# Twelve single buffers for the pair mask, and 28 pair additions moved from the edge stage to the expert block

## The chip, the cores and the metric

The kernel runs on one core of one Trainium2 chip. Its parts are named as the profile names them: TensorE (PE, with PEld for its weight loads), VectorE (DVE), ScalarE (ACT), GpSimd (POOL) and SyncE (SP), which here only issues transfers. The metric is the device time of one execution in microseconds; the median of three runs is compared.

## The reference

Input: x (1250 rows of 512), 20000 edges (src, dst) with features and weights. Four blocks, each added to x. They are given here without the layer norms ahead of each.

```python
x = x + L0_gnn(norm(x), src, dst, ...)       # messages on 20000 edges, segment_sum into 1250 nodes
x = x + L0_ffn(norm(x), ...)                 # 64 experts, sign routing, splines: x + y in it
x = x + L1_gnn(norm(x), [src, dst], ...)     # 4 blocks: sparse attention and a two-layer MLP
x = x + L1_ffn(norm(x), ...)                 # ternary weights, SwiGLU
```

Inside L0_ffn (its input is the normalised x, called z below, so that x + z + y is what comes out):

```python
xn = (x - mu) * rsqrt(var + EPS) * gamma + beta
tidx = best tile of the best cluster by sign agreement
y = einsum(spline(sigmoid(xn @ Wd[tidx])), Wu[tidx]) * scale[tidx]
return x + y
```

Inside each attention of L1_gnn:

```python
scores = einsum('ehd,ehd->eh', q[src], k[dst])          # one score per edge and head
attn = softmax of the scores over the edges of one src
out = segment_sum(attn * v[dst], src)
```

An edge may occur more than once. The kernel computes this attention densely, over 1250 x 1250, with a mask: the logarithm of how often the pair (src, dst) occurs, and a huge negative number where it does not.

## The kernel before

**Order of the stages**, with the time in the profiled execution: input projection (to 90 us), edge stage (90 to 549), node_update (to 589), expert_norm (590 to 626), route (to 665), experts (665 to 955), the first rows stage (956 to 1120), then four rounds of attention and MLP and the last FFN, to 2903. Every stage is a block in which each engine has its own list of instructions in a fixed order, written by hand; between engines there are only semaphores.

**The pair counts.** The 20000 edges lie in 160 tiles (ET) of 125. For each tile one indirect transfer of POOL adds 125 counts (`late_cnt`, at `late_idx`) to a 1250 x 1250 array in HBM. There are two such arrays, `pairs0` and `pairs1`, used in turn, and an addition waits for the one two before it (`pair_adds`, line 572; it issues at line 580). Their sum is the count. The 160 additions are spread: 68 in the edge stage (EARLY_ADDS, of which 60, PACED_ADDS, by group), 14 in node_update, 78 in experts; `late_adds` (line 585) issues part k of the table LATE.

**Edge stage.** 40 groups of 4 edge tiles. POOL fetches node rows for a group two ahead (L339) and then issues its share of additions (L580). VectorE makes messages and one-hots (L427), TensorE gathers them by a one-hot product (L539).

**expert_norm.** ScalarE makes z = X * rstd + shift for ten row tiles (L800). POOL adds z to X (L733, X is then x + z). VectorE takes statistics of z and makes xf from it (L760, L763, L765).

**experts.** Weights stream from HBM on SP's queue. TensorE computes the down products, ScalarE and VectorE the splines, TensorE the up products, and the results are stored as y_d (L1063, ten issues). POOL issues the 78 additions, waits for y_stored and for all 160 additions, and gathers the rows of y_d (L1075, ten transfers). For each gathered tile VectorE adds it, scaled, to X (L1376) and takes statistics (L1379 to L1386), ScalarE makes `first_rows` (L1269, L1272).

**First rows stage** (`rows_stage`, `source == "first"`, `masks` true). TensorE: a conditioned row norm, then 24 units, q and k (12 of each, by columns 500, 374, 376, three passes of four matmuls each, L1432), then v by ten row tiles (L1441). Unit n of q or k is finished by ScalarE (`take`, L1769, L1774) and VectorE (`finish`, k: L1884); a unit's bank is free after that, and two banks alternate. Beside it the mask of ten row tiles is built and stored in `mask_d`:

- SP loads the two count tiles (`load_pairs`, L142 and L143, 112 and 13 rows), into `pair_c` and `pair_m`, four buffer pairs in turn by the table MASK_SET; a reload waits until the mask in the place is stored.
- VectorE, behind `finish(n)` where n is in COUNT_AT or COVER_AT: the sum and its maximum (`count`, L1890), then 1e30 where it is 0 (L1896) and max(count, 1) (L1897).
- ScalarE, behind `take(n)` by LN_AT: the logarithm (L1779).
- POOL subtracts (L1642): mask = -(1e30 where empty) + log, with the sign turned; SP stores it (`store_mask`).

SP also stores x and the normalised rows at the stage's beginning (`x_d`, `g_d`, 2.5 MB each); ScalarE waits for both before unit 12, whose k overwrites the place of `first_rows`. The conditioning weights, bvo and wv are loaded by `late` in the middle. VectorE splits wk into high and low before unit 12 (L1840).

Of the kernel before, what the change touches and what calls it, by code (L numbers as in the profile page):

```python
# [34 lines left out]
EARLY_ADDS = 68  # L35
PACED_ADDS = 60
# [3 lines left out]
BIG = 1.0e30  # L40
# [530 lines left out]

LATE = (EARLY_ADDS, EARLY_ADDS + 14, ET)

# [136 lines left out]
def expert_norm(nc, T, A, xf, sc, sgnT, sigs, pairs):  # L710

    tsum = T.E.tsum
    with ExitStack() as ctx:
        sb = lambda n, s, d=F32: ctx.enter_context(nc.sbuf_tensor(n, s, d))
        z = sb("z", [P, NT, D]); gam = sb("gam", [P, D]); bet = sb("bet", [P, D])
        shift = sb("en_shift", [P, NT])
        tsg = sb("tsg", [128, NX, KD])
        csum = sb("csum", [128, NCL, KD])
        names = ("gb_in stats_s std_s step z_ready z_added mid xf_ready turned signed csummed sign_step sigs_ready "
                 "scored sc_ready")  # L720
        with Stage(nc, names) as (gb_in, stats_s, std_s, step, z_ready, z_added, mid, xf_ready, turned, signed,
                                  csummed, sign_step, sigs_ready, scored, sc_ready):
            with nc.Block() as block:
# [5 lines left out]
                @block.gpsimd  # L729
                def _(pool):  # L730
                    for t in range(NT):
                        pool.wait_ge(z_ready, t + 1)
                        nc.gpsimd.tensor_tensor(T.X[:, t, :], T.X[:, t, :], z[:, t, :], ALU.add).then_inc(z_added, 1)  # L733

                @block.vector
                def _(dve):
# [10 lines left out]
                    v.scalar_tensor_tensor(shift[:], T.mv[:, :, 0], -1.0, T.rstd[:], ALU.mult, ALU.mult).then_inc(stats_s, 1)  # L747
# [41 lines left out]
                def _(act):  # L789
# [9 lines left out]
                    for t in range(NT):  # L799
                        s.activation(z[:, t, :], T.X[:, t, :], ACT.Identity, bias=shift[:, t:t + 1],  # L800
                                     scale=T.rstd[:, t:t + 1]).then_inc(z_ready, 1)
# [196 lines left out]
def experts(nc, T, A, R, xs_d, y_d, pairs, mask_d, x_d, g_d, place):  # L998

    with ExitStack() as ctx:  # L1000
# [23 lines left out]
                 "c_in c_made sin_s c_turned c_copied c_prod c_z c_h c_done")  # L1024
        with Stage(nc, names) as (x_in0, x_in1, x_in2, x_in3, x_in4, tab_in, tab_high, tab_low, cleared, turned, xt_act, xt_dve,
# [4 lines left out]
                                  c_in, c_made, sin_s, c_turned, c_copied, c_prod, c_z, c_h, c_done):  # L1030
# [8 lines left out]
            with nc.Block() as block:  # L1039
                @block.sync  # L1040
                def _(sp):
# [19 lines left out]
                    for t in range(NS_T):  # L1061
# [3 lines left out]
                                 A["L1_gnn_wq"][0:1].rearrange("a c d -> (a c) d")).then_inc(rows_in, 16)  # L1065
                    sp.wait_ge(rows_in, 64)

                @block.gpsimd
                def _(pool):
# [14 lines left out]
                    late_adds(pool, nc, T, pairs, 1)  # L1084
# [120 lines left out]
                def _(act):  # L1205
# [70 lines left out]
                def _(dve):  # L1276
# [113 lines left out]
def expert_layer(nc, T, A, xs_d, y_d, pairs, mask_d, x_d, g_d, place):  # L1390
    class R:
        pass
    with ExitStack() as ctx:
        sb = lambda n, s, d=F32: ctx.enter_context(nc.sbuf_tensor(n, s, d))
        R.slot = sb("r_slot", [P, NT], I32); R.scale = sb("r_scale", [P, NT])
        R.ring = ctx.enter_context(nc.sbuf_tensor("w_ring", [128, RG, WG, D], F32, side="right"))
# [3 lines left out]
        with ExitStack() as c2:  # L1400
            xf = c2.enter_context(nc.sbuf_tensor("xf", [P, NT, D], F32)); sc = c2.enter_context(nc.sbuf_tensor("sc", [P, NT, NX + NCL], F32))
            with ExitStack() as c3:
                sgnT = c3.enter_context(nc.sbuf_tensor("sgnT", [128, KD, N], BF16))
                sigs = c3.enter_context(nc.sbuf_tensor("sigs", [128, KD, NX + NCL], BF16))
                expert_norm(nc, T, A, xf, sc, sgnT, sigs, pairs)
# [45 lines left out]
class Map:  # L1451
# [4 lines left out]
    def __init__(self, nc, base):  # L1456
# [29 lines left out]
        self.pair_c = [at(f"pair_c{s}", 154240 + 10048 * s + 1536 * (s // 2), [P, N]) for s in range(4)]  # L1486
        self.pair_m = [at(f"pair_m{s}", 159264 + 10048 * s + 1536 * (s // 2), [P, N]) for s in range(4)]
# [8 lines left out]
MASK_TURN = tuple(MASK_SET[:t].count(MASK_SET[t]) for t in range(NT))  # L1496


def rows_stage(nc, T, M, source, sink, g_d, x_d, loads, late, bias, bqk, bvo, last=False, pairs=None, mask_d=None):
# [11 lines left out]
             "pair_in0 pair_in1 pair_in2 pair_in3 summed_up empty floor logd mask_made mask_out0 mask_out1 mask_out2 mask_out3")  # L1511
    with Stage(nc, names) as (cw_ready, cw_next, b_in, a_in, w_in, v_in, a_high, a_cut, b_high, b_cut, v_high, v_cut,
# [4 lines left out]
                              pair_in0, pair_in1, pair_in2, pair_in3, summed_up, empty, floor, logd, mask_made,  # L1517
                              mask_out0, mask_out1, mask_out2, mask_out3):
        pair_in, mask_out = (pair_in0, pair_in1, pair_in2, pair_in3), (mask_out0, mask_out1, mask_out2, mask_out3)
# [16 lines left out]
        with nc.Block() as block:  # L1536
            @block.sync
            def _(sp):
# [3 lines left out]
                def load_pairs(t):  # L1542
                    k = MASK_SET[t]
                    if MASK_TURN[t] >= 1:
                        sp.wait_ge(mask_out[k], 32 * MASK_TURN[t])
                    wide(sp, M.pair_c[k][:], counts[0][t * P:(t + 1) * P, :], pair_in[k])
                    wide(sp, M.pair_m[k][:], counts[1][t * P:(t + 1) * P, :], pair_in[k])

                def store_mask(t):
                    sp.wait_ge(mask_made, t + 1)  # L1550
                    wide(sp, mask_d[t * P:(t + 1) * P, :], M.pair_c[MASK_SET[t]][:], mask_out[MASK_SET[t]])
# [16 lines left out]
                if masks:  # L1568
                    load_pairs(0)
                    load_pairs(1)  # L1570
                    wide(sp, x_d.rearrange("(t p) d -> p t d", p=P), T.X, T.spilled)
                    wide(sp, g_d.rearrange("(t p) d -> p t d", p=P), M.first, T.spilled)
                    sp.wait_ge(T.spilled, 64)
                    load_pairs(2)
                    load_pairs(3)
                    store_mask(0)
                    store_mask(1)
                    load_pairs(4)
                    store_mask(2)
                    load_pairs(5)  # L1580
                    store_mask(3)
                    load_pairs(6)
# [1057 lines left out]
```

## Time and profile before

| | |
|---|---|
| median of three runs | 2891.27 us (2888.83 to 2891.71) |
| profiled execution | 2904.57 us |
| its span | 2902.8 us |
| mean granted clock of TensorE | 0.939 of full |
| TensorE busy | 87% of the span |
| VectorE, ScalarE, POOL busy | 65%, 47%, 41% |

How to read what follows: times are microseconds. In the table of stretches a row is "from:to length, PE busy (x instructions) PEld busy DVE busy ACT busy POOL busy, granted clock of TensorE, share of time in which the transfer engines were busy, GB/s". A row of a timeline is "start duration engine line operation out<-in xcount [idle time before <-what ended it]"; several equal ones that follow each other are put together. SPq is SP's queue, where the duration is the time for issuing. A row of waits is "engine and line waited for: total, times, longest". A row of a source line gives durations in ns, min/median/max, and the first and last start.

### The profile page before, as it was taken

What the parts mean: (1) busy time and instruction counts of PE and PEld (TensorE: products, weight loads), DVE (VectorE), ACT (ScalarE), POOL (GpSimd) and SP (SyncE); (2) the same over time, 40 slices, a digit from 0 to 9 for tenths busy, and PEclk for the clock granted to TensorE, in tenths of its full rate; (3) what the DMA queues carried; (4) which work ended last, traced back from release to release, by engine and by line L of the source; (5) the groups of instructions that cost most, each with busy time, mean ns of one, the idle gap of its engine ahead of it and who ended that gap; (6) DMA issues with size and microseconds to landing.
All of it is one profiled execution on the core that took longest, in us unless ns stands there. A gap on an engine that the chain in (4) does not pass through costs nothing. (4 is left out here: it accounts for less than half of the span.)

```text
span 2902.8 us, 38742 instructions
## 1 busy us (share of the span) xinstructions
PE 2523.5 (87%) x13585; PEld 2168.3 (75%) x13585; DVE 1878.7 (65%) x3535; ACT 1376.8 (47%) x2744; POOL 1175.7 (41%) x868
## 2 busy tenths in 40 slices
PE   3899999747775658999999999989989989998999
PEld 3687887546565547897887887878978878877997
DVE  2799999573641855777636766556776367677762
ACT  1566665421244524665435655445654356654431
POOL 2788888833776131226003234012261022363420
PEclk9999999868778779999999999999999999999999
DMA  8444344228444661102203011111022020131101
GB/s 249 87 82 89 75 83 90 19 95 276 112 115 125 180 192 55 36 18 70 69 20 87 18 54 43 61 53 35 18 56 76 25 79 27 33 93 34 55 12 35
DMA packets 171815, 220.33 MB, mean 76 GB/s; under 512 B 111530, under 2 KB 120165, under 8 KB 164204
## 3 DMA queue, kind: packets, MB, share of 16 engines
q1 hardware_dynamic: 84873, 189.35, 22.5%
q0 software_dynamic: 86752, 28.51, 5.9%
q8 instruction: 111, 1.82, 0.3%
q14 instruction: 79, 0.65, 0.1%
HBM read 177.10 MB, written 40.15 MB: 75 GB/s over the span
## 5 line engine op out<-in xcount | busy, mean ns | idle before, releaser
L2165 POOL TENSOR_SCALAR prob<-prob,rden,linked 125x1250 f32<-125x1250 f32 x160 | 223.6, 1398 | 855.9 <-DVE rden L2132 855.9
L580 POOL DMA_INDIRECT pairs<-late_cnt,late_idx x160 | 343.4, 2146 | 128.9 <-DMA pairs<-late_cnt,late_idx 85.0
L2083 ACT CAST prob_high<-ps 125x375 fp32r<-125x375 f32 (+1 forms) x480 | 230.9, 503 | 266.9 <-PE ps L2045 266.6
L2124 DVE CUSTOM_DVE_ANT_0 prob<-ps,mask 125x1250 f32<-125x1250 f32 x160 | 233.1, 1457 | 128.6 <-PE ps L2021 109.4
L2137 DVE TENSOR_TENSOR prob_low<-ps,prob_high 125x375 fp32r<-125x375 f32 (+1 forms) x480 | 269.8, 585 | 46.5 <-ACT prob_high L2083 46.5
L339 POOL DMA_INDIRECT Hg<-h_rows,dsti x160 | 230.5, 1441 | 123.0 <-issue 99.5
L2034 PE MATMUL ps<-ident,prob 125*125 125x125 f32 x1600 | 252.4, 273 | 17.2 <-POOL prob L2165 10.6
L2034 PEld LDWEIGHTS ps<-ident,prob 125*125 125x125 f32 x1600 | 232.4, 187 | 29.7 <-POOL prob L2165 22.9
L539 PE MATMUL ps<-onehot,mhi 125*128 125x512 f32 (+1 forms) x960 | 246.4, 365 | 5.5 <-DVE onehot L427 5.3
L539 PE MATMUL ps<-onehot,mlo 125*128 125x512 f32 (+1 forms) x960 | 239.7, 358 | 0.0
L2075 ACT ACTIVATE prob<-prob,top 125x1250 f32<-125x1250 f32 x160 | 214.7, 1342 | 44.9 <-DVE top L2124 35.8
L2045 PE MATMUL ps<-prob_high,v_high 125*128 125x376 f32 (+1 forms) x480 | 211.1, 440 | 4.7 <-ACT qT L2087 3.0
L2021 PE MATMUL ps<-k_high,q_high 128*125 128x512 f32 (+1 forms) x480 | 174.2, 363 | 26.2 <-DVE q_low L2113 18.9
L539 PEld LDWEIGHTS ps<-onehot,mhi 125*128 125x128 f32 x960 | 159.0, 191 | 42.2 <-issue 12.6
L539 PEld LDWEIGHTS ps<-onehot,mlo 125*128 125x128 f32 x960 | 158.0, 191 | 28.3
L2021 PE MATMUL ps<-k_low,q_high 128*125 128x512 f32 (+1 forms) x480 | 172.4, 359 | 0.0
L2021 PE MATMUL ps<-k_high,q_low 128*125 128x512 f32 (+1 forms) x480 | 171.6, 357 | 0.0
L2045 PE MATMUL ps<-prob_low,v_high 125*128 125x376 f32 (+1 forms) x480 | 169.1, 352 | 0.0
L2045 PE MATMUL ps<-prob_high,v_low 125*128 125x376 f32 (+1 forms) x480 | 169.0, 352 | 0.0
L427 DVE TENSOR_SCALAR onehot<-iota_n,srcf 125x1250 fp32r<-125x1250 int16 x120 | 120.4, 1025 | 26.0 <-PEq L72 13.8
L2310 POOL TENSOR_SCALAR neg<-raw,qsc 128x128 bf16<-128x128 f32 x132 | 78.7, 615 | 119.2 <-DVEq L2332 119.2
L2021 PEld LDWEIGHTS ps<-k_high,q_high 128*125 128x125 f32 x480 | 90.9, 189 | 47.9 <-DVE q_low L2113 20.6
(405 smaller groups left out, 5995.9 us busy)
## 6 DMA issues: line engine op xcount, KB each, us to landing
mask<-mask_d SPq DMA_DIRECT2D x40, 546.9 KB
sg_wd<-L_ffn_Wd SPq DMA_DIRECT2D x32, 512.0 KB, 6.7
w_ring<-L_ffn_Wd SPq DMA_DIRECT2D x16, 1024.0 KB, 14.3
w_ring<-L_ffn_Wu SPq DMA_DIRECT2D x16, 1024.0 KB, 6.1
pairs<-zeros POOLq DMA_DIRECT2D x18, 625.0 KB, 26.8
keyrow<-keys_d SPq DMA_DIRECT2D x40, 244.1 KB
kept<-g_d SPq DMA_DIRECT2D x40, 224.0 KB
g_d<-kept SPq DMA_DIRECT2D x30, 224.0 KB
```

The lines of the kernel that those rows point to most:

```text
L339: nc.gpsimd.indirect_dma_start(Hg[:, g % 2, j, :, :].rearrange("p c f -> p (c f)"), None, h_rows[:, :], bass.IndirectOffsetOnAxis(dsti[:, ...
L427: v.tensor_scalar(onehot[:, j, :], T.iota_n[0:P, :], srcf[:, column(g, j):column(g, j) + 1], None, ALU.is_equal).then_inc(hot_ready, 1)
L539: ins = nc.tensor.matmul(agg_chunk(T, a, c), part[:, u, j, a * 128:(a + 1) * 128], onehot[:, j, n0:n0 + nn], start=first and k == 0 and c < 2,
L580: nc.gpsimd.indirect_dma_start(pairs[a][:, :], bass.IndirectOffsetOnAxis(T.E.late_idx[:, c:c + 1], 0), T.E.late_cnt[:, c:c + 1], None, com ...
L2021: ins = nc.tensor.matmul(S(u)[0:P, n0:n0 + nn], M.qr[x][:, b % 2, i * P:(i + 1) * P], M.k[y][:, h, n0:n0 + nn], start=n == 0, stop=n == 2)
L2034: ins = nc.tensor.transpose(T.ps[0:P, 3 + s % 4, i * P:(i + 1) * P], M.prob[:, (FIRST[b] + i) % RING, j * P:(j + 1) * P], T.ident[0:P, 0:P])
L2045: ins = nc.tensor.matmul(T.ps[:, 7, 0:w], M.v[x][:, j, h * DH:(h + 1) * DH], M.pt[y][:, s % 3, 0:w], start=j == 0 and n == 0, stop=j == NT ...
L2075: s.activation(M.prob[:, u % RING, :], M.prob[:, u % RING, :], ACT.Exp, bias=M.top[:, u % RING:u % RING + 1], scale=-1.0, accum_out=M.den[ ...
L2083: s.copy(M.pt[0][:, n % 3, 0:w], T.ps[0:P, 3 + n % 4, 0:w]).then_inc(high, 1)
L2124: v.tensor_tensor_reduce(M.prob[:, r, :], S(u)[0:P, 0:N], M.mask[:, it % MASKS, :], 1.0, 3.0e38, ALU.add, ALU.min, M.top[:, r:r + 1]).then ...
L2137: v.tensor_tensor(M.pt[1][:, n % 3, 0:w], T.ps[0:P, 3 + n % 4, 0:w], M.pt[0][:, n % 3, 0:w].bitcast(F32), ALU.subtract).then_inc(low, 1)
L2165: nc.gpsimd.tensor_scalar(M.prob[:, r, :], M.prob[:, r, :], M.rden[:, r:r + 1], T.linked[:, it:it + 1], ALU.mult, ALU.mult).then_inc(norme ...
```

## The change

The changed kernel has 20 more lines; line numbers of the order rows below are each kernel's own.

- EARLY_ADDS 68 to 40, PACED_ADDS 60 to 32, and LATE has one more part: 40 additions in the edge stage, 14 in node_update, 12 in expert_norm, 94 in experts.
- X + z leaves POOL. ScalarE makes it in experts as X * (rstd + 1) + shift, ten activations before the tables; L1376 waits for each.
- x_d is stored in experts, tile by tile, after VectorE's sum, and not in the rows stage.
- The mask has twelve buffers a to m, and each tile its own pair of them and its own semaphores. Tiles 0 to 3 are loaded at once, 4 and 5 once x_d is stored; 6 to 9 wait for stores.
- Per tile VectorE makes the sum and its maximum, ScalarE log(sum + 1e-18), then Relu(-1e28 * log - 1e28), and VectorE subtracts. POOL does only two memsets.
- COUNT_AT, LOG_AT and CAP_AT place these steps, beginning at unit 3.

```diff
-EARLY_ADDS = 68
-PACED_ADDS = 60
+EARLY_ADDS = 40
+PACED_ADDS = 32
...
-LATE = (EARLY_ADDS, EARLY_ADDS + 14, ET)
+LATE = (EARLY_ADDS, EARLY_ADDS + 14, EARLY_ADDS + 26, ET)
...
 # expert_norm, POOL
-                    for t in range(NT):
-                        pool.wait_ge(z_ready, t + 1)
-                        nc.gpsimd.tensor_tensor(T.X[:, t, :], T.X[:, t, :], z[:, t, :], ALU.add).then_inc(z_added, 1)
+                    late_adds(pool, nc, T, pairs, 1)
...
 # expert_norm, VectorE
+                    v.tensor_scalar(R.gain[:], T.rstd[:], 1.0, None, ALU.add)
...
 # experts, SP
+                    for t in range(NT):
+                        sp.wait_ge(added, t + 1)
+                        wide(sp, x_d[t * P:(t + 1) * P, :], T.X[:, t, :], T.spilled)
...
 # experts, POOL
-                    late_adds(pool, nc, T, pairs, 1)
+                    late_adds(pool, nc, T, pairs, 2)
...
 # experts, ScalarE
+                    for t in range(NT):
+                        s.activation(T.X[:, t, :], T.X[:, t, :], ACT.Identity, bias=R.shift[:, t:t + 1],
+                                     scale=R.gain[:, t:t + 1]).then_inc(x_summed, 1)
...
 # experts, VectorE, ahead of L1376
+                            dve.wait_ge(x_summed, t + 1)
...
-COUNT_AT = (6, 6, 7, 8, 9, 10, 12, 14, 16, 18)
-COVER_AT = (6, 7, 8, 9, 10, 11, 13, 15, 17, 19)
-LN_AT = (7, 8, 9, 10, 11, 12, 14, 16, 18, 20)
-MASK_SET = (0, 1, 2, 3, 0, 1, 2, 3, 1, 3)
+COUNT_AT = (3, 4, 5, 6, 8, 9, 12, 13, 15, 17)
+LOG_AT = (4, 5, 6, 7, 9, 10, 13, 14, 16, 18)
+CAP_AT = (5, 6, 8, 9, 10, 11, 14, 16, 18, 19)
...
 # rows_stage, SP
-                    load_pairs(0)
-                    load_pairs(1)
-                    wide(sp, x_d.rearrange("(t p) d -> p t d", p=P), T.X, T.spilled)
+                    for t in range(4):
+                        load_pairs(t)
+                    sp.wait_ge(T.spilled, 32 * NT)
+                    load_pairs(4)
+                    load_pairs(5)
                     wide(sp, g_d.rearrange("(t p) d -> p t d", p=P), M.first, T.spilled)
...
+                    for t in range(4):
+                        store_mask(t)
+                    sp.wait_ge(mask_out[0], 32)
                     load_pairs(6)
+                    store_mask(4)
+                    sp.wait_ge(mask_out[1], 32)
+                    load_pairs(7)
                 late(sp, cw_ready, cw_next, made, a_in, unit_made, v_in)
                 if masks:
-                    load_pairs(7)
-                    store_mask(4)
                     store_mask(5)
+                    sp.wait_ge(mask_out[2], 32)
                     load_pairs(8)
...
+                    sp.wait_ge(mask_out[3], 32)
+                    sp.wait_ge(mask_out[5], 32)
                     load_pairs(9)
+                    for t in range(6, NT):
+                        store_mask(t)
...
 # rows_stage, ScalarE
+                            act.wait_ge(T.spilled, 32 * NT + 32)
+                            act.wait_ge(mask_made, 3)
...
+                    s.activation(M.pair_c[t][:], M.pair_c[t][:], ACT.Ln, bias=M.tiny[0:P, :]).then_inc(logd, 1)
+                    act.wait_ge(logd, t + 1)
+                    s.activation(M.pair_m[t][:], M.pair_c[t][:], ACT.Relu, bias=M.far[0:P, :], scale=-BIG).then_inc(capped, 1)
...
 # rows_stage, VectorE
+                        if n == CAP_AT[t]:
+                            c = M.pair_c[t][:]
+                            dve.wait_ge(capped, t + 1)
+                            v.tensor_tensor(c, M.pair_m[t][:], c, ALU.subtract).then_inc(mask_made, 1)
```

Places in v that ScalarE and VectorE write over mask buffers wait for mask_made or for a store, as before.

POOL from expert_norm to the gather, before; L733 is X + z, L875 the scatter of the rows to their experts, L580 the additions, L1075 the gather:

```order
L733 TENSOR_TENSOR X<-X,z 125x512 x10
...
L875 DMA xs_d<-xf,r_slot 1280x512 x10
...
L1083 MEMSET cw 81x1024
L580 DMA pairs<-late_cnt,late_idx 1562628x1 x78
L1075 DMA w_ring<-y_d,r_slot 125x512 x10
```

and after:

```order
L579 DMA pairs<-late_cnt,late_idx 1562628x1 x12
...
L872 DMA xs_d<-xf,r_slot 1280x512 x10
...
L1083 MEMSET cw 81x1024
L579 DMA pairs<-late_cnt,late_idx 1562628x1 x94
L1075 DMA w_ring<-y_d,r_slot 125x512 x10
```

Twelve additions stand where the ten sums stood, and sixteen more ahead of the gather.

VectorE in the k units of the first rows stage, before; L1890 is the count, L1884 the end of a k unit:

```order
L1884 SCALAR_TENSOR_TENSOR k_low_51<-ps,bqk,k_high_50 128x374
L1890 ISA pair_c1_89,pair_top_96<-pair_c1_89,pair_m1_93 125x1250
L1890 ISA pair_top_96 125x1
L1884 SCALAR_TENSOR_TENSOR k_low_51<-ps,bqk,k_high_50 128x374
L1896 TENSOR_SCALAR pair_m1_93<-pair_c1_89 125x1250
L1897 TENSOR_SCALAR pair_c1_89<-pair_c1_89 125x1250
L1884 SCALAR_TENSOR_TENSOR k_low_51<-ps,bqk,k_high_50 128x374
L1890 ISA pair_c3_91,pair_top_96<-pair_c3_91,pair_m3_95 125x1250
L1890 ISA pair_top_96 125x1
L1884 SCALAR_TENSOR_TENSOR k_low_51<-ps,bqk,k_high_50 128x374
```

and after (L1900 ends a k unit, L1908 counts, L1914 subtracts):

```order
L1900 SCALAR_TENSOR_TENSOR k_low_51<-ps,bqk,k_high_50 128x500
L1908 ISA pair_h_95,pair_top_102<-pair_h_95,pair_c_90 125x1250
L1908 ISA pair_top_102 125x1
L1900 SCALAR_TENSOR_TENSOR k_low_51<-ps,bqk,k_high_50 128x374
L1914 TENSOR_TENSOR pair_f_93<-pair_b_89,pair_f_93 125x1250
L1900 SCALAR_TENSOR_TENSOR k_low_51<-ps,bqk,k_high_50 128x374
L1908 ISA pair_g_94,pair_top_102<-pair_g_94,pair_d_91 125x1250
L1908 ISA pair_top_102 125x1
L1900 SCALAR_TENSOR_TENSOR k_low_51<-ps,bqk,k_high_50 128x374
```

The counts of tiles 8 and 9 stand one unit earlier than they did, and one subtract follows each where two operations stood.

SP's queue around the conditioning loads, before; `pair_c_91` is the fourth buffer and `mask_d<-` a store of a mask:

```order
L2183 DMA cw<-L_gnn_cond 17x1024 x3
L2201 DMA bvo<-L_gnn_bv 125x512
L2202 DMA set_b_raw<-L_gnn_wv 128x2048
L142 DMA pair_c_91<-pairs 112x1250
L143 DMA pair_c_91<-pairs 13x1250
L142 DMA pair_m_95<-pairs 112x1250
L143 DMA pair_m_95<-pairs 13x1250
L142 DMA mask_d<-pair_c_88 112x1250
```

and after:

```order
L141 DMA pair_f<-pairs 112x1250
L142 DMA pair_f<-pairs 13x1250
L141 DMA pair_b<-pairs 112x1250
L142 DMA pair_b<-pairs 13x1250
L2203 DMA cw<-L_gnn_cond 17x1024 x3
L2221 DMA bvo<-L_gnn_bv 125x512
L2222 DMA set_b_raw<-L_gnn_wv 128x2048
L141 DMA mask_d<-pair_g 112x1250
```

The loads of tile 7 stand ahead of the conditioning loads, which they followed before; those of tiles 8 and 9 still come behind.

## Rows read from the trace of the kernel before

**Rows 1.** Table of stretches: edge stage, the busiest 10 us, first rows stage.
```profile
270.00:360.00 90.00, 89.73 (x468) 73.03 (x467) 83.48 (x162) 57.32 (x149) 74.01 (x45) 1.00 0.41 82
975.00:985.00 10.00, 8.93 (x34) 7.37 (x35) 7.78 (x18) 4.61 (x10) 0.00 (x0) 0.71 0.97 326
956.00:1090.00 134.00, 83.89 (x350) 71.95 (x351) 86.45 (x130) 49.55 (x79) 36.69 (x14) 0.75 0.68 198
```

**Rows 2.** Waits of TensorE in the edge stage.
```profile
PE ps L539 <- DVE onehot L427: 5.3, 11, 0.8
```

**Rows 3.** The ten stores of y_d, and their landing.
```profile
L1063 SPq DMA_DIRECT2D y_d<-xs x10: 326/604/1043, 908.5 to 914.8; - x10
...
DMA to landing us min/median/max: 2.1/3.6/4.7
```

**Rows 4.** Timeline of POOL: expert_norm, and the end of the expert block.
```profile
598.70 13.18 POOL L733 TENSOR_TENSOR X<-X,z 125x512 f32<-125x512 f32 x10 [13.54 <-ACT z L800]
...
924.30 1.97 POOL L580 DMA_INDIRECT pairs<-late_cnt,late_idx  x1 [0.31 <-issue]
928.82 1.27 POOL L1075 DMA_INDIRECT w_ring<-y_d,r_slot  x1 [2.55 <-issue]
```

**Rows 5.** What POOL's additions waited for in the expert block.
```profile
  DMA pairs<-late_cnt,late_idx: 85.0, 30
```

**Rows 6.** Waits in the first rows stage.
```profile
DVE pair_c L1890 <- DMA pair_m<-pairs: 32.4, 6, 12.5
PE ps L1432 <- DVE k_low L1884: 31.3, 5, 11.6
```

**Rows 7.** Timeline of VectorE in the first rows stage.
```profile
1007.02 7.83 DVE L1840 TENSOR_TENSOR set_a_low<-set_a_raw,set_a_high 128x512 fp32r<-128x512 f32 x4
...
1056.50 1.46 DVE L1890 CUSTOM_DVE_ANT_0 pair_c<-pair_c,pair_m 125x1250 f32<-125x1250 f32 x1 [12.54 <-DMA pair_m<-pairs]
...
1078.43 1.46 DVE L1890 CUSTOM_DVE_ANT_0 pair_c<-pair_c,pair_m 125x1250 f32<-125x1250 f32 x1 [7.14 <-DMA pair_m<-pairs]
```

**Rows 8.** Timeline of SP's queue in the first rows stage.
```profile
961.29 6.26 SPq L143 DMA_DIRECT2D x_d<-X  x1
...
1047.63 0.32 SPq L142 DMA_DIRECT2D pair_c<-pairs  x1
```

**Rows 9.** Timeline of VectorE in expert_norm and beside the gather.
```profile
607.27 3.49 DVE L760 SCALAR_TENSOR_TENSOR xf<-z,mv,gam 125x512 f32<-125x512 f32 x2
610.68 1.75 DVE L763 SCALAR_TENSOR_TENSOR xf<-xf,rstd,bet 125x512 f32<-125x512 f32 x1
...
613.02 0.74 DVE L763 SCALAR_TENSOR_TENSOR xf<-xf,rstd,bet 125x512 f32<-125x512 f32 x1
...
936.62 0.72 DVE L1376 SCALAR_TENSOR_TENSOR X<-w_ring,r_scale,X 125x512 f32<-125x512 f32 x1
```

**Rows 10.** Timeline of ScalarE in expert_norm and in the expert block.
```profile
597.80 7.16 ACT L800 ACTIVATE z<-X,en_shift,rstd 125x512 f32<-125x512 f32 x10 [0.72 <-DVE en_shift L747]
...
693.49 3.60 ACT L1228 CAST tab<-sel 128x4096 fp32r<-128x4096 f32 x1 [16.18 <-DMA sel<-L_ffn_splines]
```

**Rows 11.** Timeline of TensorE: last q unit, first k unit, first v tile.
```profile
1011.28 0.85 PE L1432 MATMUL ps<-y_low,set_b_high 128*128 128x376 f32 x4
1011.97 0.85 PE L1432 MATMUL ps<-y_high,set_b_low 128*128 128x376 f32 x4
1018.18 2.00 PE L1432 MATMUL ps<-y_high,set_a_high 128*128 128x500 f32 x4 [5.37 <-ACT qT L1769]
...
1089.57 1.09 PE L1441 MATMUL ps<-set_b_high,y_high 128*125 128x512 f32 x4
```

**Rows 12.** Groups of ScalarE in the first rows stage.
```profile
L1779 ACT ACTIVATE pair_c<-pair_c 125x1250 f32<-125x1250 f32 x10 | 12.5, 1247 | 44.9 <-DVE pair_c L1897 44.9
...
L1779 ACT ACT_TABLE_LOAD x1 | 1.3, 1283 | 0.0
```

**Rows 13.** Transfers of the first rows stage in all.
```profile
DMA packets 7946, 26.54 MB, mean 162 GB/s; under 512 B 1256, under 2 KB 1256, under 8 KB 7682
```

More of the change, by code:

```diff
@@ L707, with expert_norm @@
 NGRP = OVERS + NX // WG
-def expert_norm(nc, T, A, xf, sc, sgnT, sigs, pairs):
+def expert_norm(nc, T, A, xf, sc, sgnT, sigs, R, pairs):
     tsum = T.E.tsum
@@ L1404, in expert_layer @@
                 sigs = c3.enter_context(nc.sbuf_tensor("sigs", [128, KD, NX + NCL], BF16))
-                expert_norm(nc, T, A, xf, sc, sgnT, sigs, pairs)
+                expert_norm(nc, T, A, xf, sc, sgnT, sigs, R, pairs)
             route(nc, T, A, xf, sc, xs_d, R, pairs)
@@ L1542, in load_pairs @@
                 def load_pairs(t):
[L1543 to L1547, printed above, removed]
+                    wide(sp, M.pair_c[t][:], counts[0][t * P:(t + 1) * P, :], pair_in[t])
+                    wide(sp, M.pair_m[t][:], counts[1][t * P:(t + 1) * P, :], pair_in[t])
                 def store_mask(t):
                     sp.wait_ge(mask_made, t + 1)
-                    wide(sp, mask_d[t * P:(t + 1) * P, :], M.pair_c[MASK_SET[t]][:], mask_out[MASK_SET[t]])
+                    wide(sp, mask_d[t * P:(t + 1) * P, :], M.pair_c[t][:], mask_out[t])
                 if source == "attn":
@@ L1637, in _ @@
                 if masks:
-                    for t in range(NT):
-                        c, m = M.pair_c[MASK_SET[t]], M.pair_m[MASK_SET[t]]
-                        pool.wait_ge(empty, t + 1)
-                        pool.wait_ge(logd, t + 1)
-                        nc.gpsimd.tensor_tensor(c[:], m[:], c[:], ALU.subtract).then_inc(mask_made, 1)
+                    nc.gpsimd.memset(M.tiny[:], TINY).then_inc(consts, 1)
+                    nc.gpsimd.memset(M.far[:], -BIG).then_inc(consts, 1)
             @block.tensor
@@ L1777, in logarithm, with logarithms @@
                 def logarithm(t):
-                    act.wait_ge(floor, t + 1)
-                    s.activation(M.pair_c[MASK_SET[t]][:], M.pair_c[MASK_SET[t]][:], ACT.Ln).then_inc(logd, 1)
+                    if t == 0:
+                        act.wait_ge(consts, 2)
+                    act.wait_ge(counted, t + 1)
+                    s.activation(M.pair_c[t][:], M.pair_c[t][:], ACT.Ln, bias=M.tiny[0:P, :]).then_inc(logd, 1)
+                    act.wait_ge(logd, t + 1)
+                    s.activation(M.pair_m[t][:], M.pair_c[t][:], ACT.Relu, bias=M.far[0:P, :], scale=-BIG).then_inc(capped, 1)
+                def logarithms(n):
+                    for t in range(NT) if masks else ():
+                        if n == LOG_AT[t]:
+                            logarithm(t)
                 if source == "attn":
@@ L1805, in _ @@
                 take(4)
+                logarithms(4)
                 take(5)
                 high(NT - 1)
+                logarithms(5)
                 for n in range(6, len(order)):
                     take(n)
-                    for t in range(NT) if masks else ():
-                        if n == LN_AT[t]:
-                            logarithm(t)
+                    logarithms(n)
                     if n == 7 and three:
@@ L1923, in _ @@
                 low(NT - 1)
+                masking(4)
+                masking(5)
                 for n in range(6, len(order)):
                     finish(n)
-                    for t in range(NT) if masks else ():
-                        if n == COUNT_AT[t]:
-                            count(t)
-                        if n == COVER_AT[t]:
-                            cover(t)
+                    masking(n)
                     if n == 7 and three:
```

87 lines of the change are left out of this document (42 added, 45 removed).

## The prediction

> **What bounds the kernel now.** I read the table of stages first, then the waits of TensorE, then the timelines of the two engines around the places that the diff touches. Only five stages are touched, so the 1780 us behind 1120 us stand as they are.
>
> The edge stage belongs to TensorE: in a stretch of 90 us it is busy for 89.73, at full clock, while POOL is busy for 74.01 [rows 1]. In the whole stage TensorE waits 5.3 us for the one-hots of VectorE, in eleven pieces [rows 2]. The 68 additions that POOL issues there lie under that.
>
> In the expert block the end is set by something else. The ten stores of y_d, the last thing that hangs on the products, are issued from 908.5 to 914.8 and each lands some 3.6 us later, 4.7 at most [rows 3]. POOL however issues additions until 924.30 + 1.97 = 926.27, and only then starts the gather, at 928.82 [rows 4]. The gather needs both; y_d is there by some 919.5 us, the additions by 928.8. So the additions are the bound, with some 9 us to spare on the other side. From the gather on a chain of row sums and statistics on VectorE and ScalarE ends at 955 us.
>
> In the first rows stage TensorE is busy for 83.89 of 134 us [rows 1]. It waits 31.3 us for the low part of k [rows 6], and that is VectorE standing in line: it counts the pairs of a tile between two units of k, and the count waits for its load, 32.4 us in six pieces. The longest is 12.54, the last 7.14; with one between them they make 26.4 [rows 7]. The loads are late because a buffer must be counted, logged, subtracted and stored before the ring has a place: the reload for tile 7 is issued at 1047.63 [rows 8], and its count starts at 1056.50, 12.54 us after VectorE was free for it.
>
> **Part 1: additions into the expert block, a loss.** Sixteen more additions stand ahead of the gather (78 to 94). Each takes 1.97 us and the next starts 0.30 later [rows 4], so 2.27 us each. The waits for landing, 85.0 us in thirty pieces [rows 5], belong to the time of the weight streams; sixteen additions appended at the end, from 926 on, stand in a quiet time. 16 x 2.27 = **+36.4 us**. The bounds: 34, if a piece of the early waits was made by pacing and shrinks, and 40, if one or two waits like the average of those thirty (2.8 us) come with them. Below nothing is excluded, since the gather waits for all of them and had nothing later than the additions. The spare 9 us on the other side only grow.
>
> **Part 2: twelve additions in expert_norm, and X + z gone from POOL.** 12 x 2.27 = 27 us from 590 on, over by about 617 us; the stage ends at 626, so they cost 0. If that cover were gone (a slow landing in between), each further us past 626 would count. What goes is POOL's ten adds X + z, 13.18 us from 598.70 [rows 4]. Beside them the first operations of VectorE's xf chain are stretched: two L760 take 3.49 and one L763 1.75, later ones 0.74 each at a pace of 0.66 [rows 9]. 5.24 - 3 x 0.67 = **-3.2 us**, bounds -4 and 0. The row of 3.49 shows VectorE slowed while POOL adds two tensors in SBUF. The Trainium skill, page "SBUF — State Buffer", section "Who interferes with whom", says that a VectorE instruction with two SBUF inputs contends with a GpSimd instruction that reads SBUF; by that the additions, which read their indices from SBUF, might stretch the same operations, and the sum would be 3 us higher. The row beside the gather speaks against it: POOL issues its ten indirect transfers there, and VectorE's sum of X takes 0.72 all the same [rows 9].
>
> X + z comes back on ScalarE in the expert block as ten activations like those of z, 7.16 us for ten [rows 10], in a place where ScalarE waits 16.18 us for the table of splines [rows 10]: **0**. Without that cover they cost 7. The wait that VectorE gets for it is answered 240 us before it is asked. The small VectorE operation for the gain costs 0.1 and goes with the rest.
>
> **Part 3: 28 additions out of the edge stage.** TensorE is the bound; what can come back is the wait for VectorE's one-hots, 5.3 us [rows 2]. The additions behind the last fetch are fewer, but the stage does not wait for them. **-1 us**, bounds -5 and 0.
>
> **Part 4: x_d stored tile by tile at the end of the experts.** Twenty issues of SP of some 0.4 us each against a chain of sums and statistics of under 2 us per tile (27 us for ten): SP keeps pace. The last store is issued at the end of the last sum, behind nothing, and the stage waits for its issue, not its landing. **+1 us**, bounds 0 and +4. It leaves the rows stage with 2.5 MB less in its busiest time, when SP was held for 6.26 us by its queue for the x_d store alone [rows 8]; that is counted in part 5.
>
> **Part 5: the mask, a gain.** Four things change in the rows stage.
> First, the loads. Twelve buffers let tiles 0 to 3 load at once and 4 and 5 as soon as x_d is stored; only 6, 7, 8 and 9 reuse a place. Of the six waits the three early small ones (6 us together) go; of the three long ones (26.4) I expect half to stay, since tiles 7 to 9 still wait for stores of tiles 1 to 3, behind which the store of tile 4 or 5 and the conditioning loads sit in SP's queue. The stores of the first tiles are issued only after mask 0 to 3 are made. 32.4 becomes about 19: **-13 us**.
> Second, VectorE's splitting of wk took 7.83 us for four (0.68 each when alone) and TensorE waited 5.37 us for the start of k [rows 7, 11]. With POOL no longer subtracting beside it, 7.83 becomes 2.7: **-5**.
> Third, where POOL subtracts (36.69 us of work in the stage [rows 1]) four more operations of VectorE are stretched, by some 8 us in all by my reading of the timeline; half of it lies in a wait that I have counted: **-4**.
> Fourth, new work. ScalarE gets a Relu of 125x1250 per tile, as long as its Ln, 1.25 us [rows 12], 12.5 us in all on an engine that is busy for 49.55 of 134 [rows 1]. VectorE trades two operations of 0.80 against one subtract of two 1250-wide inputs, for which the count with its two inputs and 1.46 us [rows 7] is the nearest row: nothing. The chain of a tile becomes count, Ln, Relu, subtract on two engines that also serve the k units in between, so a third of the Relu time shows: **+4**. Whether Ln and Relu share a table no row of this stage tells. Ln and the Identity of the units do: one load for ten Lns. Two loads per tile would be 26 us on ScalarE at the 1.28 us of that one, and bring the part above 0.
> The sum of part 5 is **-18 us**. The lower end is TensorE's own pace: the q units end at 1012.8; a unit of 376 columns is three passes that start 0.69 us apart, 2.07, one of 500 then 2.75; four and eight of them take 27.6 us, so v could start at 1040.4 instead of 1089.57 [rows 11], -49. That includes the clock: behind a wait a pass of 500 columns takes 2.00 us [rows 11] where 0.85 x 500/376 = 1.13 would do at full clock, the granted clock of the stage being 0.75 [rows 1]. The upper end is 0, or +7 with tables. What the transfers allow lies between: the stage moves 26.5 MB, 24 without x_d. At the 326 GB/s of its busiest 10 us that is 73 us, at its mean of 198 it is 121 [rows 1, 13]. I lean to the weak side because stores still gate loads. My band is -5 to -32.
> The Trainium skill, page "DMA: Bandwidth & Descriptors", section "Specifications", gives about 358 GB/s of HBM for a core; by that the 24 MB would take 67 us (an estimate from that page), and the gain would be nearer to the lower end, which is the first rival. The rows show 326 in the best 10 us.
>
> **The sum.** 36.4 - 3.2 + 0 - 1 + 1 - 18 = **+15 us**. The profiled run took 2904.57, span 2902.8, and lies 13.3 above the median of 2891.27; the difference of two kernels does not depend on that, so the forecast is 2891.27 + 15 = **2906 us**.
>
> **Rivals.**
> Rival A, faster: the twelve buffers take every load wait off VectorE and TensorE runs the k units at its own pace. For it: transfers are busy for only 0.68 of the stage [rows 1], so it was the ring that held them. Against it: loads 7 to 9 wait for stores, and the conditioning and wv loads stand between. It decides if pair loads 7 to 9 are in before k units 15 to 17. Rows stage -46: 36.4 - 3.2 - 1 + 1 - 46 = -13, **2878 us**.
> Rival B, no change: two thirds of it, rows stage -31; 36.4 - 3.2 - 31 - 1 + 1 = +2, **2893 us**. The band around it is that of part 5's strong side.
> Rival C, slower still: the ring was not the limit. The count of a tile may wait behind Ln and Relu, or the tables are reloaded, and the rows stage keeps its time: +33, **2924 us**. Against it: the 12.54 us behind a load issued at 1047.63 [rows 7, 8].
> That the moved additions cost nothing, because something else held the gather, I exclude by the 2.55 us between the last addition and the gather [rows 4].
>
> **How the numbers follow.** Forecast 0.59, rival A 0.16, rival B 0.17, rival C 0.08. A measurement of this kernel tells 0.2%, 5.8 us, from no change. Faster: rival A, 0.16. Same: rival B and a small share of its neighbours, 0.19. Slower: 0.65. The range reaches from 2883, inside rival A's upper side, to 2920, where part 1 is at 40 and part 5 at -5.
>
> **What would show it.** In the profile after: the last addition of the expert block ends near 963 us, less 4, and the gather follows by 2.5; the edge stage ends where it did within 5 us; VectorE's L760 row at 0.7 throughout; the waits for pair loads near 19 us; v starting some 116 us after the stage does, against 134 now; ScalarE with one table load in the mask. I am wrong if the additions overlap with something that waits anyway, or if v starts under 105 us or over 130 us after the stage's begin.

## The result, and the profile after

| | before | after |
|---|---|---|
| median | 2891.47 us (2888.83 to 2899.4, 5 runs) | 2919.34 us (2908.93 to 2922.7, 5 runs) |
| ratio | 1 | 1.0083 (95%: 1.0065 to 1.0101) |
| span of the profiled run | 2902.8 us | 2917.5 us |

The change makes the kernel 24 us slower by the ratio (19 to 29 by its interval); the two medians lie 28 us apart. The forecast was 2906 with a range to 2920, so the direction held, and the measured median of 2919.34 is inside the range by less than 1 us. The profile page of after begins like this:

```profile
span 2917.5 us, 38762 instructions
...
PE 2514.7 (86%) x13585; PEld 2160.6 (74%) x13585; DVE 1853.5 (64%) x3526; ACT 1398.0 (48%) x2764; POOL 1131.0 (39%) x850
```

The profiled run of before was 13 us above its median. A second profile of the same kernel (`r_before_again` below, span 2889.8) is nearer to its usual time, so places are compared with that one. The line that TensorE's first product of node_update leaves in the timeline, first of before in the second profile, then of after:

```profile
550.35 1.22 PE L672 MATMUL ps<-agg,nu_w 64*128 64x512 f32 x1 [7.66 <-DMA nu_w2v<-L_gnn_w_f2o_v]
```

```profile
542.89 1.22 PE L671 MATMUL ps<-agg,nu_w 64*128 64x512 f32 x1 [5.47 <-DMA nu_w2v<-L_gnn_w_f2o_v]
```

The edge stage gave back 7.5 us, more than the 1 forecast. In the first profile this row stood at 556.90; 6.5 us of the 13 were lost there.

The additions in expert_norm, in POOL's timeline of after, and beside them VectorE's xf chain. Both are the rows that answer to [rows 4] and [rows 9]:

```profile
595.25 2.39 POOL L579 DMA_INDIRECT pairs<-late_cnt,late_idx  x1 [0.31 <-issue]
597.94 10.31 POOL L579 DMA_INDIRECT pairs<-late_cnt,late_idx  x1 [0.30 <-issue]
608.55 1.96 POOL L579 DMA_INDIRECT pairs<-late_cnt,late_idx  x1 [0.30 <-issue]
610.82 1.97 POOL L579 DMA_INDIRECT pairs<-late_cnt,late_idx  x1 [0.30 <-issue]
615.84 0.18 POOL L864 IOTA w<- 125x64 f32 x1 [3.05 <-POOLq L71]
```

```profile
593.06 1.42 DVE L757 SCALAR_TENSOR_TENSOR xf<-z,mv,gam 125x512 f32<-125x512 f32 x2
594.39 0.75 DVE L760 SCALAR_TENSOR_TENSOR xf<-xf,rstd,bet 125x512 f32<-125x512 f32 x1
...
605.65 0.75 DVE L762 SCALAR_TENSOR_TENSOR xf<-xf,rstd,bet 125x512 f32<-125x512 f32 x1
```

VectorE is at full pace (0.75 per operation, 1.42 for two where [rows 9] has 3.49), as forecast. But one addition lasts 10.31 us: it is held from the middle of the chain to 2 us after the chain's last operation. Two more follow, and the stage ends with POOL at 612.8, not with the xf chain at 606.4. Route begins 9.4 us behind the last xf; before it was 2.8.

The end of the expert block, timeline of POOL and the waits of the 94 additions, for [rows 4] and [rows 5]:

```profile
950.54 1.96 POOL L579 DMA_INDIRECT pairs<-late_cnt,late_idx  x1 [0.30 <-issue]
955.09 1.27 POOL L1075 DMA_INDIRECT w_ring<-y_d,r_slot  x1 [2.58 <-issue]
```

```profile
L579 POOL DMA_INDIRECT pairs<-late_cnt,late_idx x94: 1960/1977/3895, 658.6 to 950.5; - x94
...
  DMA pairs<-late_cnt,late_idx: 82.0, 25
```

And the waits of the first rows stage (line, what it waited for: total, times, longest), for [rows 6]:

```profile
PE ps L1437 <- DVE k_low L1900: 20.8, 4, 14.4
...
DVE pair_h L1908 <- DMA pair_c<-pairs: 15.1, 1, 15.1
...
PE ps L1437 <- ACT qT L1771: 7.5, 4, 3.5
DVE pair_j L1908 <- DMA pair_a<-pairs: 6.1, 1, 6.1
...
DVE pair_f L1908 <- DMA pair_b<-pairs: 5.1, 1, 5.1
```

```profile
SPq L141 <- DVE pair_a L1914: 19.3, 1, 19.3
SPq L141 <- DMA cw<-L_gnn_cond: 13.0, 1, 13.0
```

Three waits for pairs are left, 26.3 us in all against 32.4; the longest grew from 12.5 to 15.1. v begins 119.8 us after the stage (982.48 to 1102.31), in the second profile of before 131.4 us.

The ledger between the second profile of before and that of after, by landmarks of the timelines:

| stretch | forecast | measured |
|---|---|---|
| edge stage, to the first product of node_update | -1 | 542.89 - 550.35 = -7.5 |
| xf chain of expert_norm | -3.2 | -3.1 |
| from there to route: additions in expert_norm | 0 | +6.6 |
| route, start of experts | 0 | +1.0 |
| experts, to the gather (sixteen more additions) | +36.4 | +41.1 |
| gather to the rows stage (x_d stores) | +1 | +0.8 |
| rows stage, to v | -18 | -11.5 |
| all that follows | 0 | +0.3 |
| sum | +15 | +27.7 |

### The profile page after: what moved, and what is told of

Same layout as the page of the kernel before. It is cut to its first block and busy times, and to the rows that moved or that the text cites. A ratio compares the mean times of both kernels' runs of the same rounds, so it can differ in the third digit from the quotient of the medians.

```text
span 2917.5 us, 38762 instructions
## 1 busy us (share of the span) xinstructions
PE 2514.7 (86%) x13585; PEld 2160.6 (74%) x13585; DVE 1853.5 (64%) x3526; ACT 1398.0 (48%) x2764; POOL 1131.0 (39%) x850
## 5 line engine op out<-in xcount | busy, mean ns | idle before, releaser
L338 POOL DMA_INDIRECT Hg<-h_rows,dsti x160 | 223.7, 1398 | 181.3 <-DVEq L449 92.2
L1678 PE MATMUL ps<-cwr,condT 81*125 81x512 f32 x160 | 56.4, 435 | 106.7 <-DVE cwr L1919 83.2
L426 DVE TENSOR_SCALAR onehot<-iota_n,srcf 125x1250 fp32r<-125x1250 int16 x120 | 110.9, 946 | 24.6 <-PEq L71 12.4
```

Source lines behind the costliest of these rows:

```text
L338: nc.gpsimd.indirect_dma_start(Hg[:, g % 2, j, :, :].rearrange("p c f -> p (c f)"), None, h_rows[:, :], bass.IndirectOffsetOnAxis(dsti[:, ...
```

## The experiments

All ratios are to the kernel before on the same chip, with their 95% intervals; 1% is 29 us.

**The first profile of before.** `r_before_again` is before, unchanged.

> The kernel before, once more. Its profiled run was 13 us above its median. Theory E (the 14 us that the edge stage seems to have gained are a hitch of that one profiled run of before): here TensorE starts node_update's first product near 545 us, 10 or more earlier than the 556.90 of the first profile. Rival (the edge stage really gains 14 us by losing 28 additions): again near 556.

Measured: 2891.54 us, span 2889.8, and the row 550.35 above. The expected 545 was half right: 6.5 of the 14 us between the first two profiles were a hitch, 7.5 were real.

**The two halves apart.** `e_adds_only` has the additions and X + z moved, the old mask and the old x_d:

```diff
-EARLY_ADDS = 68
+EARLY_ADDS = 40
-LATE = (EARLY_ADDS, EARLY_ADDS + 14, ET)
+LATE = (EARLY_ADDS, EARLY_ADDS + 14, EARLY_ADDS + 26, ET)
```

> The kernel before with the 28 additions moved (40 edge, 14 node_update, 12 expert_norm, 94 experts) and X + z on ScalarE; mask and x_d as before. My sum: +36 (gather) -3 (xf) -1 (edge) = +32 us, 2923. With the stall of expert_norm seen in the profile after (the addition issued at 597.94 lasted 10.31 us, route began 6.6 us later than it could) and an edge gain of 1: +39, 2930. Rival, edge gain of 14 real: +25, 2916.

Measured: 1.0115 (1.0099 to 1.013), +33 us.

`e_mask_only` has the other half: everything of the change but the places of the additions.

```diff
-LATE = (EARLY_ADDS, EARLY_ADDS + 14, EARLY_ADDS + 26, ET)
+LATE = (68, 82, 82, 160)
```

> The changed kernel with 68 additions in the edge stage, 14 in node_update, none in expert_norm and 78 in experts, as before; buffers, x_d and X + z as changed. My sum: -3 (xf) -14 (rows stage, by the profile after) + 0 to 2 (tail) = -16 us, 2875. If most of it came from the additions being elsewhere: about 2890.

Measured: 0.9951 (0.9938 to 0.9963), -14 us. The halves sum to +19, the whole is +24. X + z on ScalarE and its 3 us are in both halves, which brings the sum to +22, and the intervals leave room for the rest. The part of the change about the mask is a gain, the additions cost more than twice as much. The end of the expert block with 94 additions in `e_adds_only`, then with 78 in `e_mask_only`, in POOL's timeline:

```profile
949.69 1.96 POOL L580 DMA_INDIRECT pairs<-late_cnt,late_idx  x1 [0.30 <-issue]
954.27 1.27 POOL L1073 DMA_INDIRECT w_ring<-y_d,r_slot  x1 [2.62 <-issue]
```

```profile
910.99 1.96 POOL L579 DMA_INDIRECT pairs<-late_cnt,late_idx  x1 [1.74 <-DMA pairs<-late_cnt,late_idx]
916.32 1.27 POOL L1075 DMA_INDIRECT w_ring<-y_d,r_slot  x1 [3.37 <-DMA pairs<-late_cnt,late_idx]
```

**The stall in expert_norm.** `e_norm0` takes its twelve additions out and puts them back into the edge stage; experts keep their 94.

```diff
-LATE = (EARLY_ADDS, EARLY_ADDS + 14, EARLY_ADDS + 26, ET)
+LATE = (52, 66, 66, 160)
```

> The changed kernel with the twelve additions of expert_norm put back into the edge stage (52 edge, 14, 0, 94 experts). Theory N (an addition in expert_norm is held while VectorE runs its two-input operations, and the stage waits for POOL): 6 to 7 us under the changed kernel, route begins about 3 us after the last xf. Rival (no cost there, as I predicted): the same as the changed kernel within 2 us.

Measured: 1.0059 (1.0044 to 1.0074), 7 us under the changed kernel. Route begins 2.8 us after xf's last operation. That fits theory N and not my forecast of 0. Node_update's first product starts at 543.40 with 52 additions in the edge stage, as with 40.

`e_norm5` leaves 68 in the edge stage and puts five in expert_norm, where they end before the xf chain begins.

```diff
+LATE = (68, 82, 87, 160)
```

> The changed kernel with 68 additions in the edge stage, 14, 5 in expert_norm and 73 in experts. Theory N (only an addition issued beside the chain of two-input operations is held): no addition over 3 us, route begins 3.5 us after the last xf. The gather then waits for y_d rather than for additions: 3 to 9 us under e_mask_only, 2870 to 2876. Rival (additions in expert_norm cost by their number): about 3 us for the five.

Measured: 0.9902 (0.9882 to 0.9922), 2870.94 us. That is 8 us under `e_mask_only` by the medians and 14 by the ratios; in the profiles the rows stage begins 7.8 us earlier. Its fourth and fifth addition in expert_norm, then its last addition and its gather:

```profile
593.27 1.97 POOL L579 DMA_INDIRECT pairs<-late_cnt,late_idx  x1 [0.30 <-issue]
595.55 1.96 POOL L579 DMA_INDIRECT pairs<-late_cnt,late_idx  x1 [0.30 <-issue]
```

```profile
896.34 1.98 POOL L579 DMA_INDIRECT pairs<-late_cnt,late_idx  x1 [0.30 <-issue]
908.99 1.27 POOL L1075 DMA_INDIRECT w_ring<-y_d,r_slot  x1 [10.68 <-DMA y_d<-xs]
```

No addition is held, and the gather now waits 10.68 us for y_d, not for additions. So five before the xf chain cost nothing, and of twelve one was held beside it: this points to the position and not the number. That VectorE's two-input operations hold it is an inference from where it begins and ends; the additions beside the statistics chain (one input, 584 to 592 in after) took 1.97 us each. The two additions ahead of the held one also ran beside the xf chain, in 1.97 and 2.39 us, which no run explains.

**How many additions the edge stage bears.** `e_edge76` has 76 there, and 65 in experts.

```diff
+EARLY_ADDS = 76
+PACED_ADDS = 68
+LATE = (76, 90, 95, 160)
```

> The changed kernel with 76 additions in the edge stage, 14, 5 and 65. Theory P (POOL has 17 us of slack in the edge stage at 68 additions and each costs 2.4): node_update begins 5 to 10 us later than with 68, at most 3 us of it come back in the experts, since y_d ends them; 3 to 8 us slower than e_norm5. Rival (TensorE alone bounds the edge stage, as I predicted): the same as e_norm5.

Measured: 0.9925 (0.9903 to 0.9947), not told apart from `e_norm5`. Node_update's first product starts at 551.93 against 551.36; in nine of the ten profiles with 68 additions it starts from 550.4 to 553.4 (in the first of before at 556.9), in the three with 40 or 52 from 542.9 to 543.7. Theory P fell: eight more additions cost nothing that stands out of that spread, though sixteen fewer (52) gain 7 to 8. The kernel has a step there, not a slope. The waits behind the stage show one piece of it: TensorE waits for the weights of node_update 5.4 us with 40 or 52 additions, 7.7 with 68, 9.5 with 76. SP issues these weights 0.8 us after TensorE's last product with 40 additions (538.2 against 537.4), but 3.0 us after it with 68 (545.7 against 542.7), and 3.8 us after the end of the last addition at 541.9. What makes up the rest is open.

**x_d.** `e_xd_back` is `e_mask_only` with x_d stored in the rows stage.

```diff
-                        wide(sp, x_d[t * P:(t + 1) * P, :], T.X[:, t, :], T.spilled)
+                    wide(sp, x_d.rearrange("(t p) d -> p t d", p=P), T.X, T.spilled)
```

> e_mask_only with x_d stored in one piece in the rows stage, as before, ahead of the loads of tiles 4 and 5. Part 4 of my prediction alone: 1 to 2 us back at the end of the experts. What the rows stage loses by 2.5 MB more in its first 30 us: 0 if the loads of tiles 0 to 3 go first and nothing later is late, 3 to 6 if tiles 4 and 5 come late. Together -2 to +5 us against e_mask_only.

Measured: 0.9935 (0.9915 to 0.9955), the same as `e_mask_only` within the intervals. Gather to rows stage is 26.7 us, against 28.3; v begins 120.9 us after the stage, against 120.5. Where x_d is stored is worth 1 to 2 us and no more.

**What the last long wait in the rows stage is.** `e_cw_wait` is `e_mask_only` with SP's wait for the conditioning loads (cw) at the stage's end:

```diff
                 sp.dma_start(flat(M.raw_b), one(par("wv", L))).then_inc(v_in, 16)
-                sp.wait_ge(cw_next, 48)
...
+                if three:
+                    sp.wait_ge(cw_next, 48)
```

> The kernel with the new mask and the old places of the additions (e_mask_only, 2879 us), and SP's wait for the landing of the conditioning loads moved to the end of the rows stage, so that the loads of tiles 8 and 9 no longer stand behind it. Theory W (the one long wait for pairs that is left, 15.0 us, comes from the 13.0 us that SP waits there): load 8 goes out some 12 us earlier, the 15.0 becomes 2 to 5, 10 us under e_mask_only, 2869. Rival (the transfers are full and the load lands no earlier): the same within 2 us.

Measured: 0.996 (0.9945 to 0.9975), no gain. The load of tile 8 was issued 12 us earlier (80 us into the stage, not 92), and VectorE waited as long:

```profile
1022.22 0.43 SPq L141 DMA_DIRECT2D mask_d<-pair_g  x1
1022.69 0.40 SPq L142 DMA_DIRECT2D mask_d<-pair_g  x1
1023.13 5.23 SPq L141 DMA_DIRECT2D pair_h<-pairs  x1
```

```profile
1047.26 1.46 DVE L1910 CUSTOM_DVE_ANT_0 pair_h<-pair_h,pair_c 125x1250 f32<-125x1250 f32 x1 [15.91 <-DMA pair_c<-pairs]
```

Theory W fell, but not for its rival's reason: the transfer engines were busy for only 0.14 of 1035 to 1045, and for 0.07 of 1038 to 1043, which is about one engine of sixteen. The next three runs test whether the conditioning loads hold that one. A cw load is 17 rows of 4 KB; `e_cw_split` is `e_norm5` with each in two issues.

```diff
-                sp.dma_start(T.cw[r:r + CH + 1, :, :]..., one(par(f"cond{k}", L))).then_inc(cw_in, 16)
+                sp.dma_start(T.cw[r:r + CH, :, :]..., one(par(f"cond{k}", L))[0:CH]).then_inc(cw_in, 16)
+                sp.dma_start(T.cw[r + CH:r + CH + 1, :, :]..., one(par(f"cond{k}", L))[CH:CH + 1]).then_inc(cw_in, 16)
```

> e_norm5 with each of the three conditioning loads (17 rows of 4 KB) issued as 16 rows and 1 row. In the first rows stage of the kernels so far the transfers run at about 26 GB/s and a busy share near 0.06, one engine of sixteen, for 7 to 8 us before the late loads of pairs go out or land; 3 x 68 KB at 26 GB/s are 8 us. Theory Q (17 rows go through a single transfer engine, and what is issued later has pieces behind them there): the tail vanishes, SP's wait of 13 us for the conditioning loads falls to 3 to 6, the 15.3 us for the pairs of tile 8 to 5 to 8; 7 to 10 us under e_norm5. Rival (the tail is of something else, the 1 MB of wv or the row that is sent to 125 partitions): the same within 2 us.

The busy share of the transfer engines in tenths and the rate, 1000 to 1060 us in 40 slices, of `e_norm5` and then of `e_cw_split`:

```profile
DMA  8499999999999952000199999999959304839000
GB/s 243 173 300 187 273 230 233 357 357 213 217 228 204 270 182 101 27 25 27 58 299 204 283 243 243 237 230 237 303 217 320 120 11 133 280 90 303 27 0 0
```

```profile
DMA  5779899999999999999999996930393900000000
GB/s 163 250 213 243 227 230 260 307 397 257 247 207 232 264 286 337 257 300 243 223 237 240 227 317 258 320 113 0 117 290 113 300 13 0 0 0 0 0 11 0
```

The stretch at 25 to 27 GB/s with a busy share of 0 tenths (slices 17 to 19) is gone. The packets of the two traces show why. The three loads are 51 packets of 4096 bytes. In `e_norm5` they run one behind the other from 1018.8 to 1028.6, at the end in 0.16 us each while nearly nothing else runs; in `e_cw_split` up to nine of them run at a time, and all are done within 4.8 us. The waits of `e_cw_split`:

```profile
PE ps L1437 <- DVE k_low L1900: 14.7, 4, 7.7
...
DVE pair_h L1908 <- DMA pair_c<-pairs: 8.0, 1, 8.0
```

```profile
SPq L141 <- DMA cw<-L_gnn_cond: 7.8, 1, 7.8
```

SP waits 7.8 instead of 13.1 us, VectorE 8.0 instead of 15.3, and v begins 113.7 us after the stage instead of 121.0. Theory Q holds in the stage, though SP's wait fell less than to the 3 to 6 that it expected. The whole kernel does not show it: 0.9918 (0.9901 to 0.9934), where 7 us would have made 0.988.

`e_cw_both` has the split and the late wait.

> e_norm5 with the split of e_cw_split and SP's wait for these loads at the end of the stage as in e_cw_wait. Theory Q: now the early issue counts too, since nothing of load 8 stands behind a crowded engine: 3 to 5 us under e_cw_split. Rival: the transfers are full at 270 GB/s then, and it is the same as e_cw_split within 2 us.

Measured: 0.9923 (0.9901 to 0.9945); v 113.9 us after the stage. The late wait adds nothing, as its rival says.

`e_before_split` is before with the split alone.

> The kernel before with nothing changed but the conditioning loads in 16 rows and 1 row. Its longest wait for pairs (12.5 us) ended a load that SP issued after 12.8 us of waiting for these loads. Theory Q: 7 to 9 us under before, that is most of what the twelve buffers gained (11 us in the rows stage). Rival (in before the ring of four pairs is the limit by itself, as I predicted): 0 to 3 us.

Measured: 0.9988 (0.9973 to 1.0003), v 126.3 us after the stage instead of 131.4. So 5 us in the stage, between the two theories. The longest wait for pairs in the second profile of before, 12.21 us for tile 7, became 5.32; the two waits behind it (6.46 and 6.64) stayed. The ring was a limit of its own, and a part of what I had put down to it was this load.

`e_best_again` is `e_cw_both` once more:

> The kernel of e_cw_both once more, in more rounds, since the 7 us that the split took off the first rows stage did not show in the time of the whole (0.9918 and 0.9923 of before, against 0.9902 for e_norm5). If they are real for the whole: 0.987 to 0.989 of before. If they are given back behind the stage, or smaller than the spread of the rest: 0.990 to 0.993.

Measured: 0.9909 (0.989 to 0.9927), in the second of the two ranges. The part behind the first rows stage, from the load of wo (`set_a_raw<-L_gnn_wo`) to the end, took 1775 to 1787 us in all fourteen profiles; 1780 in `e_norm5`, 1785, 1781 and 1787 in the three that have the new mask and the split, 1775 in `e_before_split`. Whether the split itself costs there, or that is the spread of that part, stays open. The fastest are `e_norm5`, `e_cw_split` and the kernel of `e_cw_both` and `e_best_again` (0.990 to 0.992), 22 to 28 us under before, and some 50 under the change as it was made. The runs don't tell them apart.

## Why the prediction was right, and where it was not

**What bounds the kernel** was read rightly where it decided: the gather waits for the additions, and all sixteen more came out at its time. The **+36.4** was +41.1, outside its bounds of 34 and 40. The price of an addition at the end was right (2.28 us, 948.26 to 950.54). The missing 4.7 us are waits: 75.0 us for landings in 25 pieces and 2.5 put down to y_d in the second profile of before, 82.0 in 25 with 94 additions. The first profile of before, on which I counted, has 85.0. The **9 us to spare** on the side of y_d were 6: with 73 or 65 additions the gather starts 248.9 us after the block's first addition, with 78 in `e_mask_only` 255.0.

**Part 2** had its gain (-3.1 for -3.2) and missed a loss. The failed step is "they cost 0, over by about 617 us": the cover was argued by length alone, not by what VectorE does there. I had looked at who slows whom in one direction only. [rows 9] shows VectorE slowed beside a POOL operation; the run showed POOL held for 10.31 us beside VectorE. The Trainium skill's page "SBUF — State Buffer", section "Who interferes with whom", says that "Issue order, not op shape, decides who blocks", and that descriptor generation is starved when GpSimd does not get its port. I weighed only its other half and set it aside by a gather whose neighbours alternate with statistics and small operations. This trace agrees that one of the two can be blocked, and the 6.6 us by which route is late are its price. It does not agree with the section in full. The section infers that an operation with two SBUF inputs takes the read side only, which descriptor generation does not need, and says that the ports are held for one instruction; here the addition was held over thirteen operations of 0.75 us.

**Part 3** was -1 with bounds -5 and 0, and measured -7.5. The failed step is that only TensorE's waits for one-hots could come back, and that the stage does not wait for the last additions. 3.9 us of those waits went (5.7 to 1.8). 2.2 us more were the wait for node_update's weights. SP issues their loads at the end of the stage, and with 68 additions that end comes 3.8 us after the last of them (ending at 541.9 in the second profile of before, 548.5 in the first), 3.0 us after TensorE is done. 1.4 us are unexplained.

**Part 4** held: +0.8, and 1 to 2 by `e_xd_back`.

**Part 5** went the way and in the order I gave, but with -11.5 for -18. The term that was mis-sized is the first, -13 for the loads. Six waits did become three, but they sum to 26.3 us and not 19: -6. I explained the 12.54 us wait by the ring of four. It was for the larger part the conditioning load ahead of it (12.21 to 5.32 us with the split alone), which the change leaves in place: split there too, it brings v 7.3 us earlier (`e_norm5` to `e_cw_split`), and mask and split together bring v 17.7 us earlier than in before. -5 for wk held in kind (2.50 for four instead of 7.83), and Ln and Relu share a table, as the one load in ScalarE's timeline shows. Ln and Relu take 1.34 each. The terms -4 (other stretched operations) and +4 (the Relu) were not measured apart; the rest adds up without them, -6 and -5 for the measured -11.5.

Of the **rivals**, none came: A (TensorE's pace) had the right objection against it, the loads 7 to 9. C's time of 2924 lies nearer to the result than the forecast, but its mechanism (nothing gained in the rows stage) is refuted by `e_mask_only`. The sum's errors were -6.5, +6.6, +1.0, +4.7, -0.2, +6.5 and some tenths. The first two cancel by luck: had the edge stage given back only the 1 us that I gave it, the time would have left the range. Parts 1, 2 and 3 all came out beyond their own bounds. The range's upper end was added up wrongly too: with part 1 at 40 and part 5 at -5 the sum gives +32 and 2923, not 2920.

## What to carry to other kernels

Work that is moved from a stage where its engine has slack into one where others wait for that engine costs its full price: ask first who waits for the last of it. Where two stages are compared, take two profiles of the kernel before, since one may carry a hitch larger than the term in question. A wait that ends with a transfer is not yet explained by when the transfer was issued: look at the busy share of the transfer engines. Here 0.07 of sixteen was one engine that still worked on an earlier load.

## What the runs showed of the hardware

An addition by indirect transfer, 1.97 us when alone, took 10.31 us in two kernels (after and `e_adds_only`), both times across a chain of VectorE operations with two inputs in SBUF and ending 1.9 us behind it; next to one-input statistics it took 1.97. That the chain holds it is inferred from these times, and two additions earlier beside the same chain took 1.97 and 2.39.

Three loads of 17 rows (3 x 68 KB) ran at 27 GB/s at the end, with a busy share of the transfer engines of 0.07 (`e_norm5`, 1024.5 to 1028.5) and their packets one behind the other. As 16 rows and 1 row the tail vanished. The Trainium skill's page "DMA: Bandwidth & Descriptors", section "Why a DMA increments its semaphore by 16 and not by 1", says that a transfer is spread over the largest number of engines up to 16 that divides the slowest dimension of both sides. By that 17 rows go to one engine, and this trace agrees, with the share of 0.07, near one sixteenth.
